# Block and value transfers in other pieces, and own instruction sequences for the first unit and the last four half groups of an attention kernel

## The reference

```python
q, k, v = proj(Wq), proj(Wk), proj(Wv)            # x @ W.T, split into heads
scores = einsum('bhsd,bhtd->bhst', q, k) * D ** -0.5
attn = softmax(where(mask, -inf, scores))
out = (attn @ v, heads joined) @ Wo.T
xn = out / sqrt(mean(out * out) + 1e-6) * rms_scale
xn = xn * (1 + sc[b]) + shift[b]                  # from silu(cond) @ Wc.T + bc
x = x + xn
x = x + rotated(x)                                # fixed 4x4 mix of the four column blocks
```

## Time and profile before

| | us |
|---|---|
| median of 3 runs | 828.29 (827.21 to 829.35) |
| the profiled execution's own time | 826.24 |
| its span (first to last instruction) | 824.4 |
| TensorE busy | 799.9 (97%) |
| ScalarE, VectorE, GpSimd busy | 605.8, 606.6, 517.5 |
| stage one ends, first tile of stage two is transposed | about 261 |
| values of group 0 start | 279.1 |
| values of group 29 start | 754.3 |
| values of the last half group start | 803.8 |
| end | 824.4 |

### The profile page before, as it was taken

The page is one execution under the profiler, slowest core; times in us unless marked ns, Lnnn a source line. Parts: engine busy times, 40 slices in busy tenths (PEclk is TensorE's granted clock), DMA queues, the critical chain, the costliest instruction groups (busy, mean ns, idle before and its releaser), DMA issues.

```text
span 824.4 us, 16423 instructions
## 1 busy us (share of the span) xinstructions
PE 799.9 (97%) x4864; PEld 597.2 (72%) x4864; DVE 606.6 (74%) x1495; ACT 605.8 (73%) x1504; POOL 517.5 (63%) x375
## 2 busy tenths in 40 slices
PE   9999999999998999999999999998999999999887
PEld 6788888888887776677677767775677677767664
DVE  4612313213227899999999999999899999997666
ACT  6222222323326899999999999999999999998772
POOL 0899992000000111288888887888788888888984
PEclk9999999999999899999999999999999999999999
DMA  8964555546388888999998999898989998998001
GB/s 286 339 222 179 204 188 207 191 155 227 128 307 290 288 279 287 331 336 322 324 319 307 305 322 334 291 307 293 321 304 336 328 313 295 327 319 294 27 27 52
DMA packets 116912, 216.63 MB, mean 263 GB/s; under 512 B 12360, under 2 KB 13000, under 8 KB 116832
## 3 DMA queue, kind: packets, MB, share of 16 engines
q1 hardware_dynamic: 116688, 215.42, 76.4%
q10 hardware_dynamic: 144, 0.26, 0.1%
HBM read 133.81 MB, written 81.82 MB: 262 GB/s over the span
## 4 chain that ended last, share of the span: by engine, by line
ACT 21%; PE 16%; POOL 10%; issue 8%; DMA 7%; DVE 3%; SPq 3%; DVEq 0%; ACTq 0%; POOLq 0%
ACT probs L156 15%; PE banks L831 5%; DMA blocks_scratch<-blocks 5%; ACT turned_probs L1074 5%; PE banks L866 4%; POOL late L711 4%; PE banks L137 4%; DMA turned_probs<-blocks_scratch 3%; POOL late L1212 2%; SPq L749 1%; PE banks L900 1%; PE banks L880 1%; ACT o_T L1106 1%; DVE blocks L956 1%; ACT inv_T L1090 1%
## 5 line engine op out<-in xcount | busy, mean ns | idle before, releaser
L156 ACT ACTIVATE probs<-probs,least 128x512 f32<-128x512 f32 x512 | 376.3, 775 | 3.1 <-DVE least L148 3.1
L148 DVE CUSTOM_DVE_ANT_0 probs<-banks,mask_bias 128x512 f32<-128x512 f32 x512 | 327.7, 681 | 11.3 <-PE banks L137 9.9
L831 PE MATMUL banks<-ident,probs 128*128 128x128 f32 x1568 | 232.0, 274 | 0.0
L831 PEld LDWEIGHTS banks<-ident,probs 128*128 128x128 f32 x1568 | 191.9, 141 | 43.2 <-issue 6.7
L137 PE MATMUL banks<-k_rows,q_rows 128*128 128x512 f32 x496 | 201.4, 456 | 5.8 <-DVE least L148 5.8
L1074 ACT ACTIVATE turned_probs<-banks 128x512 f32<-128x512 f32 x256 | 159.6, 643 | 16.9 <-PE banks L831 11.9
L419 DVE SCALAR_TENSOR_TENSOR late<-banks,late 128x512 fp32r<-128x512 f32 x64 | 44.0, 690 | 160.0 <-ACT late L356 160.0
L156 ACT ACTIVATION_READ_ACCUMULATOR probs<-probs,least 128x1 f32 x512 | 129.8, 254 | 0.0
L711 POOL TENSOR_TENSOR late<-rot,late 128x2048 f32<-128x2048 f32 x28 | 128.9, 4604 | 0.0
L356 ACT ACTIVATE late<-banks 128x512 fp32r<-128x512 f32 x64 | 38.2, 598 | 119.3 <-PE banks L492 113.7
L866 PE MATMUL banks<-turned_probs,v_sb 128*32 128x512 f32 (+1 forms) x1088 | 116.9, 570 | 9.1 <-DMA turned_probs<-blocks_scratch 7.6
(11 more groups left out here) (136 smaller groups left out, 1331.9 us busy)
## 6 DMA issues: line engine op xcount, KB each, us to landing
q_rows<-q_scratch SPq DMA_DIRECT2D x128, 256.0 KB, 4.7
k_rows<-k_scratch SPq DMA_DIRECT2D x124, 256.0 KB, 4.9
blocks_scratch<-blocks SPq DMA_DIRECT2D x120, 256.0 KB, 5.2
turned_probs<-blocks_scratch SPq DMA_DIRECT2D x120, 256.0 KB, 3.4
q_scratch<-late SPq DMA_DIRECT2D x64, 256.0 KB, 2.3
k_scratch<-late SPq DMA_DIRECT2D x64, 256.0 KB, 2.3
v_sb<-v_scratch SPq DMA_DIRECT2D x8, 1024.0 KB, 7.8
out<-late SPq DMA_DIRECT2D x29, 256.0 KB, 5.7
```

The costliest lines, as they stand in the source:

```text
L148: dve.tensor_tensor_reduce(self.probs[:, n % RING, :], self.ps[:, n % SCORE_BANKS, :], self.mask_bias[:, c, :], 1.0, 3e38, ALU.add, ALU.mi ...
L156: act.activation(self.probs[:, n % RING, :], self.probs[:, n % RING, :], ACT.Exp, bias=self.least[:, n % 32:n % 32 + 1], scale=-1.0, accum ...
L831: last = pe.transpose(turn_bank("tile", n)[:, j * P:(j + 1) * P], probs[:, n % RING, j * P:(j + 1) * P], ident[:, :])
```

## The change

It moves the same data and makes the same number of instructions on TensorE, in another order.

- `EARLY`: ten tiles instead of nine, in four lots after projections 3, 4, 5 and 6.
- `move_blocks`: the four writes are cut by `k` over all 128 partitions (still 256 KB each), and the reads are two of 512 KB, issued when all four writes have landed. The semaphore `moved` becomes two.
- `load_v`: for batches 2 to 7 four pieces of 256 KB, one each at the end of groups g = 1, 2 and 3 of batch b - 1 and one at the start of g = 0 of batch b, ahead of its `move_blocks`. `load_mod(0)` goes from ahead of group 4's work to behind its `load_unit`.
- The first unit has its own tables ("first"): the four block transposes stand at places 3, 5, 8, 9 instead of 1, 2, 2, 3, and ScalarE copies out 11 of the 12 turned tiles instead of 8 (`BY_ACT`).
- Each half group has its own tables. Values stand at place 3 or 2 instead of 1, `rescale` at 2, 3, 2, 4 instead of 1 (2 in the last).
- In the half groups the residual addition is done by VectorE (`residual`) at places 2, 3, 4, 5, and no longer by GpSimd (`add`).

```diff
-EARLY = ((4, range(0, 3)), (5, range(3, 6)), (6, range(6, 9)))
-EARLY_END = 9
+EARLY = ((3, range(0, 3)), (4, range(3, 6)), (5, range(6, 9)), (6, range(9, 10)))
+EARLY_END = 10
-BLOCKS_AT = (1, 2, 2, 3)
+BLOCKS_AT = {"first": (3, 5, 8, 9), "early": (1, 2, 2, 3), "whole": (1, 2, 2, 3)}
-VALUES_AT = {'early': 2, 'whole': 2, 'half': 1}
+VALUES_AT = {"first": 2, "early": 2, "whole": 2, "half0": 3, "half1": 2, "half2": 2, "half3": 2}
-BY_ACT = {'early': '1--0--1011011011', 'whole': '1--0--1011011011', 'half': '01010011'}
+BY_ACT = {"first": '1--1--1110111111', "early": '1--0--1011011011', "whole": '1--0--1011011011', "half0": '01111111', "half1": '00111110', "half2": '11110010', "half3": '00011011'}
+SQUARE_AT = {"first": 1, "early": 0, "whole": 0, "half0": 1, "half1": 1, "half2": 1, "half3": 2}
+RESCALE_AT = {"first": 1, "early": 3, "whole": 3, "half0": 2, "half1": 3, "half2": 2, "half3": 4}
+RESIDUAL_AT = {"half0": 2, "half1": 3, "half2": 4, "half3": 5}
...
             def move_blocks(v):
                 sp.wait_ge(blocked, TC * (v + 1))
                 if v >= 2:
-                    sp.wait_ge(moved, 16 * TC * (v - 1))
-                for a in (0, 2, 1, 3):
-                    sp.dma_start(scr["blocks"][v % 2, a].rearrange("(k p) t -> p k t", p=D),
-                                 blocks[a * D:(a + 1) * D].rearrange("p k j c t -> p k (j c t)")).then_inc(blocks_out[a], 16)
+                    sp.wait_ge(moved[v % 2], 32 * (v // 2))
+                to = scr["blocks"][v % 2].rearrange("a (k p) t -> a p k t", p=D)
+                for k in range(TC):
+                    sp.dma_start(to[:, :, k], blocks[:, k].rearrange("p j c t -> p (j c t)")).then_inc(blocks_out[k], 16)
                 if v >= 2:
                     sp.wait_ge(valued, v - 1)
-                for a in (0, 2, 1, 3):
-                    sp.wait_ge(blocks_out[a], 16 * (v + 1))
-                    sp.dma_start(turned_probs[:, HG * v % SLOTS, a, :], scr["blocks"][v % 2, a]).then_inc(moved, 16)
+                for k in range(TC):
+                    sp.wait_ge(blocks_out[k], 16 * (v + 1))
+                for a in range(0, TC, 2):
+                    sp.dma_start(turned_probs[:, HG * v % SLOTS, a:a + 2, :],
+                                 scr["blocks"][v % 2, a:a + 2].rearrange("a p t -> p a t")).then_inc(moved[v % 2], 16)
...
                 if v == NG:
                     sp.wait_ge(held_made, TC)
-                    load_v(1)
-                    load_mod(0)
+                    load_v(1, slice(0, TC))
...
+                if g == 0 and b >= 2:
+                    load_v(b, slice(TC - 1, TC))
                 if chunks == ALL:
                     move_blocks(v)
...
+                if v == NG:
+                    load_mod(0)
                 if g == 0 and b > 0:
                     load_mod(b)
-                if g == 1 and 0 < b < B - 1:
-                    load_v(b + 1)
+                if g > 0 and 0 < b < B - 1:
+                    load_v(b + 1, slice(g - 1, g))
...
+            def residual(m):
+                dve.wait_ge(scaled_ready, m + 1)
+                dve.wait_ge(shifted, m + 1)
+                dve.tensor_tensor(x_of(m), x_of(m), acc[:, m % 2], ALU.add).then_inc(summed, 1)
...
-                if v > NG:
+                if NG < v <= POOL_GROUPS:
                     add(v - NG - 1)
```

More of the change, by code:

```diff
@@ L49 @@
 FIRST = [sum(SIZE[:v]) for v in range(V + 1)]
-KIND = ["early"] * NG + ["whole"] * (U - 2 - NG) + ["half"] * 4
+KIND = ["first"] + ["early"] * (NG - 1) + ["whole"] * (U - 2 - NG) + ["half0", "half1", "half2", "half3"]
 GROUP_OF = {(u, c): v for v, (u, chunks) in enumerate(GROUPS) for c in chunks}
-VALUES_AT = {'early': 2, 'whole': 2, 'half': 1}
[L53 to L62, removed]
@@ L63 @@
-BY_ACT = {'early': '1--0--1011011011', 'whole': '1--0--1011011011', 'half': '01010011'}
+VALUES_AT = {"first": 2, "early": 2, "whole": 2, "half0": 3, "half1": 2, "half2": 2, "half3": 2}
+SCALE_TURN_AT = {"first": 4, "early": 4, "whole": 4, "half0": 3, "half1": 2, "half2": 3, "half3": 2}
+INVERT_AT = {"first": 2, "early": 1, "whole": 1, "half0": 1, "half1": 0, "half2": 0, "half3": 1}
+SPREAD_AT = {"half0": 3, "half1": 2, "half2": 0, "half3": 1}
+SCALE_OUT_AT = {"first": 1, "early": 4, "whole": 4, "half0": 4, "half1": 3, "half2": 3, "half3": 4}
@@ new lines @@
+NORM_AT = {"first": 6, "early": 6, "whole": 6, "half0": 2, "half1": 3, "half2": 2, "half3": 3}
+HI_AT = {"half0": 5, "half1": 4, "half2": 6, "half3": 6}
+LO_AT = {"half0": 6, "half1": 4, "half2": 6, "half3": 7}
+SCORES = {"first": (0, 2, 3, 0, 0, 0, 0, 0, 0, 1, 1, 1, 2, 3, 2, 1),
+         "early": (1, 2, 1, 0, 1, 0, 0, 3, 1, 1, 1, 0, 2, 0, 2, 1),
+         "whole": (1, 2, 1, 0, 1, 0, 0, 3, 1, 1, 1, 0, 2, 0, 2, 1),
[4 rows of a table added]
+MASKS = {"first": (0, 1, 1, 1, 0, 1, 0, 1, 0, 0, 3, 0, 1, 4, 2, 1),
+         "early": (2, 3, 0, 0, 1, 1, 0, 2, 1, 2, 0, 1, 0, 1, 1, 1),
+         "whole": (2, 3, 0, 0, 1, 1, 0, 2, 1, 2, 0, 1, 0, 1, 1, 1),
[4 rows of a table added]
@@ L64 @@
+EXPS = {"first": (2, 0, 2, 0, 1, 0, 0, 0, 3, 0, 0, 2, 3, 2, 0, 1),
+         "early": (0, 6, 0, 1, 0, 0, 0, 2, 0, 2, 1, 0, 2, 0, 0, 2),
+         "whole": (0, 6, 0, 1, 0, 0, 0, 2, 0, 2, 1, 0, 2, 0, 0, 2),
[4 rows of a table added]
+BY_ACT = {"first": '1--1--1110111111', "early": '1--0--1011011011', "whole": '1--0--1011011011', "half0": '01111111', "half1": '00111110', "half2": '11110010', "half3": '00011011'}
 BY_ACT = "".join(BY_ACT[kind] for kind in KIND)
 TURNS = [n - BY_ACT[:n].count("-") for n in range(len(BY_ACT) + 1)]
-PARTS_AT = (4, 4, 5, 5, 7, 7, 10, 13, 13, 15, 15, 15)
@@ L67 @@
-HELD_AT = {c: [(c, at) for at in PARTS_AT] for c in range(TC)}
+PARTS_AT = {"first": (6, 8, 8, 9, 10, 11, 12, 13, 13, 14, 14, 15),
+         "early": (4, 4, 5, 5, 7, 7, 10, 13, 13, 15, 15, 15),
+         "whole": (4, 4, 5, 5, 7, 7, 10, 13, 13, 15, 15, 15),
[4 rows of a table added]
+SQUARE_AT = {"first": 1, "early": 0, "whole": 0, "half0": 1, "half1": 1, "half2": 1, "half3": 2}
+RESCALE_AT = {"first": 1, "early": 3, "whole": 3, "half0": 2, "half1": 3, "half2": 2, "half3": 4}
+RESIDUAL_AT = {"half0": 2, "half1": 3, "half2": 4, "half3": 5}
@@ L68 @@
+HELD_AT = {c: [(c, at) for at in PARTS_AT[KIND[c]]] for c in range(TC)}
 HELD_OUT = {(c + 1, 1): c for c in range(TC)}
@@ L70 @@
 POOL_GROUPS, LATE_X = V - 5, TC * (B - 1)
[L71 to L75, removed]
+PROJECT_AT = {m: [(m + NG, at) for at in PARTS_AT[KIND[m + NG]]] for m in range(CHUNKS + 1)}
 LATE_SHIFTS = {V - 4: (V - 4 - NG,), V - 3: (V - 3 - NG, LATE_X), V - 2: (LATE_X + 1, LATE_X + 2), V - 1: (LATE_X + 3,)}
-SQUARE = {(m + NG + 1, 0 if KIND[m + NG + 1] == "whole" else 0): m for m in range(CHUNKS - 1)} | {(V - 1, 2): CHUNKS - 1}
-RESCALE = {(m + NG + 1, 3 if KIND[m + NG + 1] == "whole" else 1): m for m in range(CHUNKS - 1)} | {(V - 1, 2): CHUNKS - 1}
+SQUARE = {(m + NG + 1, SQUARE_AT[KIND[m + NG + 1]]): m for m in range(CHUNKS)}
+RESCALE = {(m + NG + 1, RESCALE_AT[KIND[m + NG + 1]]): m for m in range(CHUNKS)}
+RESIDUAL = {(m + NG + 1, RESIDUAL_AT[KIND[m + NG + 1]]): m for m in range(V - 4 - NG - 1, CHUNKS)}
 WARM = 10
@@ L650, in attention @@
         valued, normed = sem("valued"), sem("normed")
-        blocks_out = [sem(f"blocks_out{a}") for a in range(TC)]
-        moved = sem("moved")
+        blocks_out = [sem(f"blocks_out{k}") for k in range(TC)]
+        moved = [sem(f"moved{i}") for i in range(2)]
         o_hi_ready, o_ready = sem("o_hi_ready"), sem("o_ready")
@@ L848, in values @@
                 if part == 0 and v % NG == 0:
[L849 removed]
+                    pe.wait_ge(v_in[b % 2], 16 + 64 * (b // 2))
                 if part == 0:
@@ L861, in values @@
                         if part == 0:
-                            pe.wait_ge(moved, 16 * TC * (v + 1))
+                            pe.wait_ge(moved[v % 2], 32 * (v // 2 + 1))
                         to = to.rearrange("p (c a t) -> p a c t", c=TC, a=TC)
@@ L953, in block @@
                     dve.wait_ge(projected, (TC + 2 * NG) * (B - 1) + 2 * NG)
-                for a in range(TC) if c == 0 and v > 0 else ():
-                    dve.wait_ge(blocks_out[a], 16 * v)
+                for k in range(TC) if c == 0 and v > 0 else ():
+                    dve.wait_ge(blocks_out[k], 16 * v)
                 dve.transpose(blocks[:, :, :, c, :].rearrange("p k j t -> p j k t"),
@@ L1034, in _ @@
                     masks += 1
-                for place, at in zip(BLOCK_PLACES, BLOCKS_AT):
-                    if chunks_of(v) == ALL and t == at:
+                for place, at in zip(BLOCK_PLACES, BLOCKS_AT[KIND[v]]) if chunks_of(v) == ALL else ():
+                    if t == at:
                         block(FIRST[v] + place)
@@ L1041, in _ @@
                     rescale(RESCALE[v, t])
+                if (v, t) in RESIDUAL:
+                    residual(RESIDUAL[v, t])
                 if t == NORM_AT[KIND[v]] and v > 0:
```

5 lines of the change are left out of this document (3 added, 2 removed), and 16 rows, old and new, of tables (EXPS, MASKS, PARTS_AT, SCORES).

## The result

The changed kernel takes 1057.05 us (median of 4 runs, 1053.2 to 1057.53), the one before 827.75 in the same session: ratio 1.2754, 95% interval 1.2713 to 1.2795. Predicted were 821 us and a range of 811 to 834. The profiled execution took 1056.76 us, its span is 1054.9 against 824.4, so 230.5 us are to be found.

A forecast was written before the change was run, and what follows sets the result against it. TensorE, busy 799.9 of 824.4 us, was taken as the bound, with the DMA engines nearly one; 826.2 - 1 (first unit) - 2 (middle) - 4.5 (half groups) = 818.7 profiled, 821 as median, range 811 to 834.

The forecast's parts named there:

- The writes now use all partitions: Middle, block writes: the new cut saves up to 1.2 us where the queue is empty, nothing where it is full.
- rival 3: Middle: the longer stop makes the DMA engines the bound, 17.1 us a group against 16.38, +18, 841 us in all; chance 0.14.
- The stop before the reads: Middle: both reads wait for the last landing, so the DMA engines' stop of 1.6 us becomes 3.5.
- the middle: Groups 0 to 29: waits won less longer reads and the moved modulation load, -2.0 us, bounds -8 and +18.
- With 2.7 us the sum is 16.3 and nothing is lost: Argument against the DMA engines as bound of the middle: a stop of 2.7 us leaves a group at 16.3 us.
- The values: Middle: loads in pieces remove the waits of groups 14 and 26 and part of group 18's, -3.2 us.
- load_mod(0): Middle: moved behind group 4's reads, it takes 1.4 us from ahead of them; group 4 -0.7, group 5 +1.9.
- The first unit: Start of the kernel: parted transposes and fewer mask waits, values of group 0 near 278; -1 us, between -2.6 and +1.5.
- The new places part the transposes: First unit, VectorE: the four block transposes, one piece of 2.49 us that holds the masks, get separated.
- The half groups: End of the kernel: additions on VectorE shorten GpSimd's loop from 14.0 to 12 us; -4.5 us, from -1 to -6.5.

The follow-up runs named there:

- reads_in_two: The kernel before with the blocks' reads as two of 512 KB behind all four landings, writes still cut by a: 849.68 us, ratio 1.0235.
- the fastest kernel: The kernel before with values in pieces, new half-group sequences (values of group 29 at place 1) and scratch laid out by k: 821.27 us, ratio 0.9936.
- writes_in_8: The changed kernel with each write by k cut into two of 64 partitions, outermost dimension 2: 1353.73 us, ratio 1.6341 against the kernel before.
- first_alone: The kernel before with only the first unit's new sequence and ten early tiles: 829.56 us, ratio 1.0045.
- halves_alone: The kernel before with only the four half groups' new sequences and the residual additions on VectorE: 824.15 us, ratio 0.995.

## Why the prediction was wrong

**The step that failed** is "The writes now use all partitions. [...] So the new writes save up to 3 x 0.4 = 1.2 us where the queue is empty and nothing where it is full". I looked at the side in SBUF, 128 partitions, and took the rate of the old writes, 391 GB/s, for the new. The other side's pattern has 4 elements outermost, and the rate is 102. Instead of 2.7 us the writes take 10.3. At that size my own sum for rival 3 would have read 10.3 + 3.5 + 10.9 = 24.7 us a group; measured 24.1. The form of the rival was right and its first term was four times too small. The rule on the outermost dimension stands on the page of the Trainium skill that I cited for another figure (DMA: Bandwidth & Descriptors).

**The stop before the reads** was the second error, hidden under the first. I took -2 for the middle and gave the DMA bound 0.14. `reads_in_two` costs 21.6 us by itself, near rival 3's +18. I also wrote that the range of 811 to 834 held all but the far end of that rival, while its own time was 841. "With 2.7 us the sum is 16.3 and nothing is lost" was the error: I had taken 3.5 us for the stop myself, 4.0 are measured in one group, and the sum of a mean group says nothing of those that have a load ahead; 16 groups waited.

**The values** were right as a mechanism: the waits of groups 14, 18 and 26 are gone (-4.0, taken -3.2). **`load_mod(0)`** had the wrong price: +1.9 for the queue, while TensorE waits 6.4 us by way of GpSimd and group 4 grows by 9.1. That groups 4 and 29 would wait longer was not seen.

**The first unit**: taken -1, measured +2.8 to +3.7, outside my bound of +1.5. "The new places part the transposes" is false, and no mask stands ahead of the last of them. Before, TensorE waited for masks and came to the values without a wait for their landing; without those waits it comes first, and the landing sets the start. I had computed the landing's path (near 278, measured 279.45) and counted the gain of TensorE's waits, but not the wait that takes their place nor the clock behind it.

**The half groups**: -4.5 taken, up to -6.5; the four groups give -7.1 to -7.4, by the mechanism forecast: the additions go to VectorE and GpSimd's loop gets shorter. In the kernel after, its shifts in the second and third half group, in the timeline of GpSimd:

```profile
1006.80 1.30 POOL L1214 TENSOR_TENSOR late<-late,mod_b 128x512 f32<-128x512 f32 x1
...
1019.05 3.02 POOL L1214 TENSOR_TENSOR late_x<-late_x,mod_b 128x512 f32<-128x512 f32 x2
```

12.2 us a loop, 12 forecast, 14.0 before. What I left out is the seam ahead of them, +5.5 us for q. By the medians the sequences are worth 3.9 us.

**Open:** what the half groups would take if the load of x that GpSimd waits for were issued earlier, how the 21.6 us of `reads_in_two` divide, and how much of the fastest kernel's gain is the layout of its scratch.

## What to carry to other kernels

Before a transfer is cut in another way, write down the outermost dimension of both sides' patterns and price the transfer by a row of the same shape; a share far below 1 at a steady rate with work queued is the mark of a transfer on few engines. A stop between a write and the read of it costs more than its mean, in each group that has bytes ahead of it. When waits are taken out of a schedule, ask who waits for each moved load on every engine, and look at the seams between stages, for a wait that is won inside a stage comes back there.

## What the runs showed of the hardware

The rate of a write to the scratch went with the outermost dimension of its pattern: 2 elements 51 GB/s (share 0.13), 4 elements 102 GB/s (0.27), 32 elements 391 GB/s. The issue showed it weakly: from 500 to 760 us SP took 2.4 to 3.8 us for the four writes before and 3.0 to 6.4 after, and 14.1 to 15.8 for the eight of `writes_in_8`. The loads behind such writes did not overlap them here, since SP stood waiting for the landing. TensorE's clock made waits dearer than they look: behind the 5.26 us in `first_alone` 32 matmuls took 2.6 us more (6.28 against 3.64), and of the 5.5 us that group 28 lost in `halves_alone` the wait itself was 4.55.
